# The orders of four engines turned in the loop of an adapter and quantised feed-forward kernel

## The reference

```python
y = einsum('bij,bkj->bik', x, weight[adapter_ids])           # adapter
h = layernorm(y) * gamma + beta
h = fake_quant(h) @ fake_quant(w1).T + b1                    # scale = max|row| / 127
g = gelu(h)
f = fake_quant(g) @ fake_quant(w3).T + b3
out = x + f
```

## Time and profile before

| | |
|---|---|
| time, median of 3 runs | 364.77 us (364.62 to 370.62) |
| profiled execution | 364.19 us, span 362.4 us |
| PE busy | 340.5 us (94% of the span) |
| DVE busy | 277.4 us (77%) |
| POOL busy | 266.0 us (73%) |
| ACT busy | 225.8 us (62%) |
| DMA, main queue | 67.14 MB, 70.2% of 16 engines' span |

### The profile page before, as it was taken

How to read it: one execution, slowest core, us unless ns; L and a number is a source line. 1 busy time by engine, 2 the same in 40 slices (tenths; PEclk the granted TensorE clock), 3 DMA queues, 4 the chain that set the end, 5 groups by cost and what they waited for, 6 DMA issues and landing times.

```text
span 362.4 us, 5807 instructions
## 1 busy us (share of the span) xinstructions
PE 340.5 (94%) x1880; PEld 234.0 (65%) x1880; DVE 277.4 (77%) x342; ACT 225.8 (62%) x232; POOL 266.0 (73%) x162
## 2 busy tenths in 40 slices
PE   6899999999967999999999999999999999999995
PEld 6787988757834666666666565556666665584542
DVE  1359798899927886897779785888679885839787
ACT  2434577956977558854777558754877467723860
POOL 1401359855997699967999399958999499986851
PEclk9999999999999999999999999999999999999999
DMA  6999997687922999189952999089943990050005
GB/s 192 341 327 405 404 324 157 178 231 186 240 39 72 268 215 221 39 207 281 216 107 90 294 219 204 3 237 264 219 91 108 301 248 38 1 210 25 0 2 232
DMA packets 46203, 67.35 MB, mean 186 GB/s; under 512 B 2918, under 2 KB 37734, under 8 KB 46186
## 3 DMA queue, kind: packets, MB, share of 16 engines
q1 hardware_dynamic: 46186, 67.14, 70.2%
HBM read 58.74 MB, written 8.39 MB: 185 GB/s over the span
## 4 chain that ended last, share of the span: by engine, by line
POOL 44%; issue 23%; PE 10%; DVE 9%; DMA 7%; SPq 3%; ACT 2%; POOLq 0%; DVEq 0%
POOL o L471 8%; POOL x_res L479 7%; POOL y_first L463 6%; POOL a L483 5%; POOL x_lo L488 4%; POOL y_first L465 3%; DMA w_nat<-in_L_cond_weight 3%; POOL o L474 3%; PE t_ps L1190 2%; DMA h_r<-in_L_cond_weight 2%; PE a_ps L1096 2%; PE a_ps L1098 2%; PE a_ps L1097 2%; DMA x_t<-in_L_ffn_b 2%; POOL rstd L447 1%
## 5 line engine op out<-in xcount | busy, mean ns | idle before, releaser
L1096 PE MATMUL a_ps<-w_hi,x_hi 128*128 128x512 f32 x256 | 107.1, 418 | 2.3 <-DVE w_lo L816 1.3
L1098 PE MATMUL a_ps<-w_hi,x_lo 128*128 128x512 f32 x256 | 100.2, 392 | 0.0
L1097 PE MATMUL a_ps<-w_lo,x_hi 128*128 128x512 f32 x256 | 99.8, 390 | 0.0
L1151 PE MATMUL f_ps<-w_q,q_t 128*128 128x512 bf16 x400 | 90.7, 380 | 7.2 <-ACT q_t L649 3.9
L1151 PEld LDWEIGHTS f_ps<-w_q,q_t 128*128 128x128 bf16 x400 | 37.1, 98 | 56.8 <-ACT q_t L649 8.3
L831 DVE TENSOR_TENSOR w_lo<-t_ps,w_hi 128x1024 fp32r<-128x1024 f32 x48 | 57.1, 1218 | 14.1 <-ACT w_hi L593 13.9
L825 DVE STREAM_TRANSPOSE t_ps<-w_nat 128x1024 f32<-128x1024 f32 x48 | 57.5, 1238 | 10.0 <-DMA w_nat<-in_L_cond_weight 9.6
L593 ACT ACTIVATE w_hi<-t_ps 128x1024 fp32r<-128x1024 f32 x48 | 48.3, 1020 | 24.9 <-DVE t_ps L825 24.0
L1096 PEld LDWEIGHTS a_ps<-w_hi,x_hi 128*128 128x128 f32 x256 | 48.1, 188 | 15.4 <-issue 2.8
L1098 PEld LDWEIGHTS a_ps<-w_hi,x_lo 128*128 128x128 f32 x256 | 48.0, 188 | 10.7
L1097 PEld LDWEIGHTS a_ps<-w_lo,x_hi 128*128 128x128 f32 x256 | 48.3, 189 | 8.9
(11 more groups left out here) (152 smaller groups left out, 495.4 us busy)
## 6 DMA issues: line engine op xcount, KB each, us to landing
w_nat<-in_L_cond_weight SPq DMA_DIRECT2D x96, 256.0 KB, 6.8
x_res<-in_x SPq DMA_DIRECT2D x7, 1024.0 KB, 7.4
out<-o SPq DMA_DIRECT2D x14, 512.0 KB, 3.0
x_nat<-in_x SPq DMA_DIRECT2D x24, 256.0 KB, 9.9
w_nat<-in_L_cond_weight SPq DMA_DIRECT2D x10, 512.0 KB, 8.0
w_q<-in_L_ffn_w SPq DMA_DIRECT2D x4, 512.0 KB, 7.3
h_r<-in_L_cond_weight SPq DMA_DIRECT2D x4, 512.0 KB, 6.4
w_scale_row<-in_L_ffn_w SPq DMA_DIRECT2D x3, 512.0 KB, 9.0
```

Source lines behind the costliest of these rows:

```text
L1096: pe.matmul(ps, hi, w_hi[:, u, c], start=begin, stop=False)
L1097: pe.matmul(ps, hi, w_lo[:, u, c], start=False, stop=False)
L1098: last = pe.matmul(ps, lo, w_hi[:, u, c], start=False, stop=end)
L1151: last = pe.matmul(ps[:, half, :], q[:, c, :], w[:, c, half_of(half)], start=c == 0, stop=c == CB - 1)
```

## The change

Four lists of the loop are reordered. No instruction is added, removed or altered, and the prologue, the last period and PE's list stay as they are.

- SP: the load of unit 1 of item p+2 goes ahead of the store of tile 0 of item p-1, behind which it stood. In SP's last pass (p = 6), where nothing more is loaded, nothing changes.
- POOL: `add_b1(p-1, 1)` goes ahead of `normalisers_of(p)` and `low_x(p+1, 1)`.
- ACT: `take_h` goes ahead of the splits of unit 0; `take_g(p-1, 0)` and `gelu(p-1, 1)` go ahead of `normalise(p, 0)`; the first split of unit 2 and `round_g(p-1, 1)` come between the two `normalise`; `take_g(p-1, 1)` goes ahead of `round_h(p, 0)`; `copy_y(p+1, 0)` goes ahead of both splits of unit 3.
- DVE: `transpose_x` goes to the front; `rescale1(p-1, 0)` goes ahead of the transposes of unit 1; `rescale1(p-1, 1)` goes ahead of the statistics; `scales_g(p-1, 1)` goes ahead of the first `low_w` of unit 2.

```diff
@@ SP: period(p)
-                store(p - 1, 0)
                 if not (isinstance(p, int) and p + 2 > LAST):
                     load_unit(p + 2, 1)
+                store(p - 1, 0)
                 store(p - 1, 1)
@@ POOL: period(p)
                 residual(p - 1)
+                add_b1(p - 1, 1)
                 normalisers_of(p)
                 low_x(p + 1, 1)
-                add_b1(p - 1, 1)
@@ ACT: period(p)
+                take_h(p - 1)
                 both(p + 1, 0)
-                take_h(p - 1)
                 split_x(p + 1, 0)
                 both(p + 1, 1)
                 gelu(p - 1, 0)
                 copy_y(p, 1)
                 round_g(p - 1, 0)
                 split_x(p + 1, 1)
+                take_g(p - 1, 0)
+                gelu(p - 1, 1)
                 normalise(p, 0)
+                split_w(p + 1, 2, 0)
+                round_g(p - 1, 1)
                 normalise(p, 1)
-                take_g(p - 1, 0)
-                split_w(p + 1, 2, 0)
-                gelu(p - 1, 1)
                 split_w(p + 1, 2, 1)
-                round_g(p - 1, 1)
                 scale_ffn2(p - 1, 0)
+                take_g(p - 1, 1)
                 round_h(p, 0)
-                take_g(p - 1, 1)
+                copy_y(p + 1, 0)
                 split_w(p + 1, 3, 0)
                 split_w(p + 1, 3, 1)
-                copy_y(p + 1, 0)
                 round_h(p, 1)
                 scale_ffn2(p - 1, 1)
@@ DVE: period(p)
+                transpose_x(p + 1)
                 both(transpose_w, p + 1, 0)
                 both(low_w, p + 1, 0)
-                transpose_x(p + 1)
+                rescale1(p - 1, 0)
                 both(transpose_w, p + 1, 1)
-                rescale1(p - 1, 0)
                 both(low_w, p + 1, 1)
                 scales_g(p - 1, 0, a[:, 0, :], 0)
+                rescale1(p - 1, 1)
                 statistics(p, 1)
                 mean_and_variance(p)
-                rescale1(p - 1, 1)
                 both(transpose_w, p + 1, 2)
+                scales_g(p - 1, 1, a[:, 1, :], 1)
                 low_w(p + 1, 2, 0)
-                scales_g(p - 1, 1, a[:, 1, :], 1)
                 low_w(p + 1, 2, 1)
```

## The result

The changed kernel takes 360.96 us (median of 10 runs, 359.75 to 366.1) against 366.14 for the kernel before (10 runs, among them the three shown ahead of the prediction). The ratio is 0.986, with an interval of 0.982 to 0.991: shorter by 1.4%, clear of no change, but by less than the 2% that the prediction took as the least that a measurement can tell. The time lies inside the range of the prediction and on the side that it named. The profiled execution took 359.75 us with a span of 357.9. Some executions of every kernel take over 1.5% longer than its fastest; the ratios and intervals in this document leave these out, the medians don't.

A forecast was written before the change was run, and what follows sets the result against it. A closed circle through POOL, SP's store and load, and DVE bound the kernel at 40.23 us a pass. Five passes at 38.62 save 6.45 us from 364.19: 357.7, taken as 358.0, range 355.2 to 361.8 (0.8).

The forecast's parts named there:

- the circle: POOL's finish, the store, unit 1's load, DVE's transposes, rescale1, add_b1, POOL again: said to set the old 40.23 us period.
- PE's own work: Matmuls and transposes PE needs in one pass without waits: 37.6 us, so five passes can't fall below 188.
- The new chain, 38.62: From PE's second first-layer product through rescale1, POOL's add_b1(p-1, 1) to scales, then DVE's low_w: next pass at 38.62 us.
- The first pass: First of the loop's five passes, 38.28 us before, as its state comes from the prologue: loses 0.34 us.
- The covers on ACT: ACT steps said to end in time: take_h at 5.8, normalise(0) covered by 0.4 us, copy and split by 1.0.
- `x_res`: Load that POOL's residual reads: taken at 5.9 us, landing at 13.7, no cost; slower rival 372 us, chance 0.07.
- The point of 15.2: Time into a pass by which x_res must land to delay nothing, 7.4 us after its issue.
- the price of 0.7 a pass: Cost per pass if the x_res load takes 8.1 us, landing at 15.9.
- The sum: Five passes at 38.62 make 193.1 against 199.55: 6.45 us less, from the profiled 364.19 to 357.7, taken as 358.0.
- The rivals: PE-bound 353.6 us, 0.10; slower by x_res 372, 0.07; part of the way 359.5 to 361.5, 0.14; nothing gained 364, 0.09.
- PE as the bound: Rival: POOL's chain is 1 us shorter, passes take 37.6 to 37.8, total 353.6 us; chance 0.10.

The follow-up runs named there:

- the front half: Kernel before with unit 1's load ahead of the store and only the first ACT and DVE moves (take_h, transpose_x, rescale1(0)): 357.67 us, ratio 0.978.
- spare step: Changed kernel plus one POOL step whose result nothing reads, before add_b1(p-1, 1) (in front): 361.65 us, ratio 0.984; or after it (behind): 365.01 us, 0.995.
- all but the load: Changed kernel with SP's load of unit 1 back behind the store: 362.28 us, ratio 0.988.
- POOL's move alone: Kernel before with only add_b1(p-1, 1) moved ahead of the normalisers and low_x(1) on POOL: 376.62 us, ratio 1.019.
- the copy back: Changed kernel with copy_y(p+1, 0) back behind both splits of unit 3 on ACT: 361.28 us, ratio 0.986.
- POOL back alone: Changed kernel with add_b1(p-1, 1) back behind the normalisers and low_x(1), ACT's and DVE's new orders kept: 389.55 us, ratio 1.057.

## Why the prediction was right

- **The bound and the circle.** Shown: cutting the circle in one place alone (the load) brings the whole gain, and the other three lists without that cut bring nearly as much, 194.36 us for the loop. PE's own work, put at 37.6, measured 37.8 where PE never waits (the front half).
- **The new chain, 38.62.** Measured 38.73 in three passes. Its points in pass 3, predicted and measured: `rescale1(0)` done 10.9 and 11.0; `add_b1(0)` 11.3 and 11.2; `add_b1(1)` 19.92 and 19.99 (213.92 - 193.93); end of the scales 35.69 and 35.79; next pass 38.62 and 38.73. The 0.1 is a half rescale of 0.75 us where I had half of a merged row, and hand-overs. The spare step shows that this chain is what sets the pass.
- **The first pass.** Predicted to lose 0.34 us, it lost 0.55 (38.83 against 38.28).
- **The covers on ACT.** `take_h` in time: PE's first product starts without a wait. `normalise(0)` was expected at 25.6 and ended at 25.5, 0.6 us ahead of the first scale. The copies ended at 35.3 as worked out, 2.1 ahead of the start of `low_w(3)`, with one split between; taking them back behind both splits changed nothing.
- **`x_res`.** Taken at 5.9, it took 5.1 to 5.5 with 7.0 in the first pass, where `residual` waited 0.70 us for it. The prediction had named such a wait as a sign that it was wrong. It cost nothing: it ended 14.2 us into the pass, and POOL still waited 1.12 us for the second product. The point of 15.2 and the price of 0.7 a pass were met by the kernel with all but the load (0.6 at a landing of 16.0). That the load was never too late is in part luck, for 7.4 us from issue to landing was all that it had. In the 28 passes after the first of the seven kernels with the load in front, it took up to 6.7 in 25 and 7.2, 7.3 and 7.8 in three; behind unit 1 it took 5.4 to 9.1 (the kernel before, all but the load, POOL's move alone). What made the three long is open. Unit 2 is issued 1.65 us behind it in the changed kernel (201.71 and 203.36 in pass 3), and `x_res` still landed in 5.2 us there. The Trainium skill ("DMA: Bandwidth & Descriptors", "Queues, rings and completion order") says that each DMA engine takes the descriptors of one ring in order; the 5.2 us are in line with that, but these landings, which overlap, don't show it.
- **The sum.** The loop gave 5.9 us where 6.45 was worked out. The rest of the distance to the forecast, 358.0 against 359.75 profiled, is the prologue's 1.45 us. The step that was off is the last one: I made the sum against one profiled execution, as if its prologue were the usual one, and it was not (the last section). That its clock alone makes up the distance to the other runs is not shown: beside the last experiments, the one run of the kernel before with a mean clock of 1.000 was the fastest of 13 (365.25, the others 366.2 or more), but beside the first ones a run at 0.994 took 364.52. Against 366.14, the median of the ten runs, the worked-out gain of 6.2 would have given 359.9, and 360.96 was measured.
- **The rivals.** None came, but `x_res` was near: in the kernel with the copy back, which has all other orders of the change, it landed 15.1 us into pass 4. PE as the bound (37.8) was the right number for another kernel: the one without the later moves.

## What to carry to other kernels

When engines with written-out orders feed each other in a loop, look for the closed circle that takes exactly one period, and add up its legs; cutting it in the cheapest place (here one DMA issue past a store that waits) can bring all that a large reorder brings. Before moving a step forward on an engine, ask what its input waits for: `add_b1` was moved to where it must stand still, past work that could have filled the wait. Test the parts of such a change one by one, since moves that are consistent with each other can together cost more than leaving them all out.

## What the runs showed of the hardware

The time that the prologue lost in the changed kernel lies in one product of 16 matmuls, `ffn2(0, 0)`, which the change does not touch. In the changed kernel it took 5.31 us (104.76 to 110.07), in the kernel before 3.63; the table by stretch of each:

```profile
106.00:107.00 1.00, 1.00 (x3) 0.30 (x2) 0.93 (x4) 0.09 (x1) 1.00 (x1) 0.50 0.00 0
107.00:108.00 1.00, 1.00 (x4) 0.41 (x3) 1.00 (x1) 1.00 (x1) 0.92 (x2) 0.50 0.00 0
```

```profile
104.83:108.46 3.63, 3.62 (x16) 1.48 (x16) 2.66 (x4) 2.69 (x3) 3.55 (x3) 1.00 0.00 0
```

The granted clock stood at 0.50, its lower level (1.2 GHz), for over 2 us, and then came back. PE had stood still for the same 1.16 and 1.39 us in front of that product in both kernels, so what decides whether the clock falls there stays open. Of the ten profiles, two have this product at full clock, the kernel before's and the one with the spare step in front; in the other eight it took 4.6 to 5.3 us. The kernel before's profiled execution was thus one of the exceptions. The same shows inside one execution. In the kernel with POOL's move alone, PE waited 2.05 us in front of `ffn2(0)` in pass 4 and again in pass 5; behind the first wait the clock was down to 0.50, behind the second it stayed at 1.00:

```profile
275.82 5.31 PE L1151 MATMUL f_ps<-w_q,q_t 128*128 128x512 bf16 x15 [2.05 <-ACT q_t L649]
...
317.53 3.63 PE L1151 MATMUL f_ps<-w_q,q_t 128*128 128x512 bf16 x15 [2.05 <-ACT q_t L649]
```

In the kernel with POOL back alone the wait was longer, 3.87 us, and the clock behind it fell to the same level (the mean was 0.92 in each of passes 2 to 5): there a wait of PE cost its own length and slower matmuls on top, which the expectation had not counted.
